# A selective scan on one core: TensorE makes the scan's input products from diagonals of B held in DRAM

## The chip, the cores and the metric

The kernel runs on one core of one Trainium2 chip. The metric is the device time of one execution in microseconds (us). The core has TensorE (PE in the profile, with PEld for its weight loads), VectorE (DVE), ScalarE (ACT), GpSimd (POOL) and SyncE (SP), which only issues DMAs here.

## The reference, cut to what matters

Two blocks follow each other over `x` of shape (2, 1024, 256): a conditioned linear layer that feeds a bidirectional Mamba block, and a conditioned linear layer that feeds a mixture of 8 experts, two for each token. The change touches only the scan of the Mamba block:

```python
x, z = (xz[..., :D_INNER], xz[..., D_INNER:])              # D_INNER = 512
x = silu(_causal_depthwise_conv(x, conv_w, conv_b))
x_dbl = x @ x_proj_w.T
dt = softplus(x_dbl[..., :DT_RANK] @ dt_proj_w.T + dt_proj_b)
Bm = x_dbl[..., DT_RANK:DT_RANK + D_STATE]                 # D_STATE = 16
Cm = x_dbl[..., DT_RANK + D_STATE:]
dA = jnp.exp(dt[..., None] * A)
dBx = (dt * x)[..., None] * Bm[:, :, None, :]              # the input products
h = dA_t * h + dBx_t                                       # the scan over time
y = jnp.einsum('bdn,bn->bd', h, C_t)                       # the output products and their sum
```

It is computed for two batches, forwards and backwards. Everything is float32.

## The kernel before, in words

**Units.** Channels lie on the 128 partitions, time along the free axis. The scan is cut into 256 units, `NU = NQ * SL`. `unit(i)` gives `q` (batch and direction, 4 values), `th` (half of the time axis, 512 steps), `pr` (a pair of the four channel blocks) and `n` (one of 16 states). A unit holds two channel blocks, `j` = 0 and 1, of 128x512 each. Sixteen units with the same `q`, `th`, `pr` are added up in the two PSUM banks `Y[0]` and `Y[1]` (`ps_y`), so there are 16 sums.

**What each engine does for a unit.** ScalarE (`decay`) makes two exponentials. VectorE makes the input product of block 0 into the bank `U` (`u`, L1068), runs the two scans (`second_scan` L1083 for block 1, `first_scan` L1096 for block 0), and in the units named in `OWN` also block 0's output product (`own_product`, L1108). GpSimd makes the input products of block 1 for two units at once (`u`, L1360, or L1356 for one) and the output products (`product`, L1376 for both blocks, L1372 for one). SP loads rows of B and C from the DRAM scratch `bc_scratch`, broadcast to 128 partitions, into a ring of three places of two units (`ring_load`). TensorE adds the output products up (`add`).

**Turned sums and flipped units.** For all but the last half of `q` = 3, `add_blocks` adds a product as four transposes of 128 columns for each block (L472): the bank holds the sum turned, with time on the partitions. At the end of a sum ScalarE copies it out (`evac_turned`), TensorE turns it back (`turn_back`, L465), and ScalarE copies it again (`evac`). The last half of `q` = 3 is `turned(q, th)` false: it adds with one plain product with the identity for each block (L470). In four units of 16 from unit 16 on, `flipped(i)`, neither VectorE nor GpSimd makes the input products: ScalarE scales the turned `dt * x` by columns of B (`u_turned`, L884, four instructions), and TensorE turns the result back into the banks (`second_u` L617, `first_u` L625).

**What sets the order.** Each engine's program is written out by hand as one loop over `i`. TensorE in iteration `i` does the turning, then `side_work(i)`, then `add(i - 2)` (`LAG` is 2). `side_work` is everything else TensorE has to do beside the scan: convolutions (L378), projections (L345, L354, L364, L386, L404, L417), and tiles of the next block (`tile`, `tile_T`, `tile_lg`, L439 to L458), each put at an iteration by a table (`STEP_AT`, `CONV_SLOTS`, `TILE_AT` and so on). Its results go through two PSUM banks, 6 and 7. VectorE's share of it is `small_work(i)`, behind the scans of unit `i`. Every queue is in order.

After the scan comes the expert stage: 39 tiles, with the products of 128 columns at L720 and of 256 columns at L731.

Of the kernel before, what the change touches and what calls it, by code (L numbers as in the profile page):

```python
# [21 lines left out]
FLIP, STRIDE = 6, 3  # L22
# [7 lines left out]
OWN = (6, 9, 12, 15, 22, 25, 28, 31)  # L30

NR, NH, NP, KD, LAG, EV, NW = 3, 5, 4, 6, 2, 4, 3


def at(q, s):
    return q * SL + s
# [3 lines left out]
STEP_AT = {3: (0, 0, 1), 22: (0, 1, 0), 36: (0, 1, 1), 54: (1, 0, 0), at(1, 3): (1, 0, 1),  # L40
           at(1, 22): (1, 1, 0), at(1, 36): (1, 1, 1), at(1, 42): (2, 0, 0), at(2, 1): (2, 0, 1),
           at(2, 18): (2, 1, 0), at(2, 33): (2, 1, 1), at(2, 46): (3, 0, 0), at(2, 59): (3, 0, 1),
           at(3, 8): (3, 1, 0), at(3, 27): (3, 1, 1)}


CONV_SLOTS = {1: (24, 26, 30, 32, 38, 40, 44, 46),
              2: (at(1, 10), at(1, 12), at(1, 16), at(1, 18), at(1, 24), at(1, 26), at(1, 30), at(1, 32)),
              3: (at(1, 59), at(1, 61), at(2, 21), at(2, 23), at(2, 27), at(2, 29), at(2, 36), at(2, 38))}
CONV_AT = {9 + 2 * m_: (0, m_, 1) for m_ in range(4)}
CONV_AT |= {i: (q_, g // 2, g % 2) for q_, slots in CONV_SLOTS.items() for g, i in enumerate(slots)}  # L50
XD_AT = {19: (0, 1), 50: (1, 0), 52: (1, 1), at(1, 38): (2, 0), at(1, 40): (2, 1), at(2, 42): (3, 0), at(2, 44): (3, 1)}
# [3 lines left out]
X1_AT = {0: (0, 1, 0), 1: (0, 1, 1), 56: (1, 0, 0), 57: (1, 0, 1), 59: (1, 1, 0), 60: (1, 1, 1)}  # L55
IN_AT = {5 + m_: (0, m_, 1) for m_ in range(4)}
IN_AT |= {i: (1, k // 2, k % 2) for k, i in enumerate((62, 63, at(1, 1), at(1, 2), at(1, 5), at(1, 6), at(1, 8), at(1, 9)))}

GATE_AT = {at(1, 44): (0, 1, 0), at(1, 45): (0, 1, 1), at(1, 49): (0, 1, 2), at(1, 50): (0, 1, 3),
           at(2, 3): (0, 0, 0), at(2, 4): (0, 0, 1), at(2, 8): (0, 0, 2), at(2, 9): (0, 0, 3),  # L60
# [3 lines left out]
LATE_AT = {at(2, 57): 0, at(2, 61): 1, at(3, 6): 2, at(3, 10): 3}  # L64
YG_AT = {g + 3: x for g, x in GATE_AT.items() if g + 3 < NU}
XT_AT = {at(1, 56): (0, 1), at(2, 15): (0, 0), at(3, 42): (1, 1), at(3, 55): (1, 0)}
XT_NO = {(0, 1): 2, (0, 0): 3, (1, 1): 4, (1, 0): 5}
OUT_AT = {at(1, 55): (0, 1, 0), at(1, 56): (0, 1, 1), at(2, 14): (0, 0, 0), at(2, 15): (0, 0, 1),
          at(3, 41): (1, 1, 0), at(3, 42): (1, 1, 1)}
TILE_AT = {at(2, 49): (0, 4), at(2, 53): (0, 5), at(2, 62): (0, 6), at(3, 2): (0, 7),  # L70
           at(3, 11): (0, 0), at(3, 15): (0, 1), at(3, 19): (0, 2), at(3, 23): (0, 3),
           at(3, 46): (1, 4), at(3, 50): (1, 5), at(3, 54): (1, 6), at(3, 58): (1, 7)}
# [4 lines left out]
def flipped(i):  # L77

    return i >= 16 and i % 16 >= FLIP and (i % 16 - FLIP) % STRIDE == 0


def flips(i):

    return sum(flipped(k) for k in range(i + 1))


def plain(i):

    return i + 1 - flips(i)


def swapped(i):

    return i + 1 < NU and flipped(i + 1)


NF = (15 - FLIP) // STRIDE + 1
DU_AT = {16 * g + 1 + j: (g, j) for g in range(1, 16) for j in range(2)}
ROWS_AT = {max(at(q_, 32 * h_), 16 * (1 - q_ - h_)) + 3: (q_, h_) for q_ in range(NQ) for h_ in range(2)}


def turned(q, th):

    return not (q == NQ - 1 and th)
# [8 lines left out]
def build(nc, d, out):  # L113
    ctx = ExitStack()
    with ctx:  # L115
# [25 lines left out]
        PS = Y + [DU, U] + DE + P2  # L141

        X_dram = nc.dram_tensor("X_scratch", (NB * T, C), F, kind="Internal").ap()
        bc_dram = nc.dram_tensor("bc_scratch", (NB * 2, 2 * NS, T), F, kind="Internal").ap()

        arena = sb("arena", [128, 43 * T + 8 * PAD + T + 64])
        am = Arena(arena)
# [135 lines left out]
        def own(i):  # L283

            return i % 32 in OWN

# [1354 lines left out]
```

## Time and profile before

| | us |
|---|---|
| median of 3 runs (1381.39 to 1389.28) | 1387.32 |
| the profiled execution | 1389.91 |
| its span, first to last instruction | 1388.1 |

| engine | busy us | share of the span |
|---|---|---|
| PE | 1228.0 | 88% |
| POOL | 918.5 | 66% |
| DVE | 899.6 | 65% |
| ACT | 777.4 | 56% |

The span has three parts: the start, up to the first scan at 41 us; the 256 units, up to about 916 us; and the experts, to the end. The shares above are averages over all three, and the stages have different limits. A record of a matmul has a duration of its own, but neighbouring matmuls overlap: the time that one takes from TensorE is read from the distance between the starts of groups, not from the mean duration.

### The profile page before, as it was taken

What the parts mean: (1) busy time and instruction counts of PE and PEld (TensorE: products, weight loads), DVE (VectorE), ACT (ScalarE), POOL (GpSimd) and SP (SyncE); (2) the same over time, 40 slices, a digit from 0 to 9 for tenths busy, and PEclk for the clock granted to TensorE, in tenths of its full rate; (3) what the DMA queues carried; (4) which work ended last, traced back from release to release, by engine and by line L of the source; (5) the groups of instructions that cost most, each with busy time, mean ns of one, the idle gap of its engine ahead of it and who ended that gap; (6) DMA issues with size and microseconds to landing.
All of it is one profiled execution on the core that took longest, in us unless ns stands there. A gap on an engine that the chain in (4) does not pass through costs nothing. (4 is left out here: it accounts for less than half of the span.)

```text
span 1388.1 us, 20902 instructions
## 1 busy us (share of the span) xinstructions
PE 1228.0 (88%) x7120; PEld 933.0 (67%) x7120; DVE 899.6 (65%) x1065; ACT 777.4 (56%) x1477; POOL 918.5 (66%) x511
## 2 busy tenths in 40 slices
PE   8978878989788879797787879898999999999997
PEld 3445555656556556566556644467999999999996
DVE  3998999899899899899998889963111111111110
ACT  4787887788887697788886675613111111111111
POOL 1998999999999989999998879822222222222211
PEclk9999999999999899899998799999999999999999
DMA  5665556465556455556555554608988898888982
GB/s 196 216 182 183 168 184 176 156 202 192 176 171 198 152 184 165 183 171 192 186 184 182 178 155 152 194 4 301 369 309 322 318 322 313 310 320 317 323 306 46
DMA packets 109979, 296.95 MB, mean 214 GB/s; under 512 B 10017, under 2 KB 21922, under 8 KB 94386
## 3 DMA queue, kind: packets, MB, share of 16 engines
q1 hardware_dynamic: 100226, 277.53, 57.9%
q0 software_dynamic: 9648, 18.09, 6.5%
q8 instruction: 57, 0.93, 0.3%
q14 instruction: 48, 0.39, 0.1%
HBM read 277.76 MB, written 9.96 MB: 207 GB/s over the span
## 5 line engine op out<-in xcount | busy, mean ns | idle before, releaser
L1376 POOL TENSOR_TENSOR arena<-arena 128x1024 f32<-128x1024 f32 x192 | 456.7, 2395 | 53.8 <-DVE arena L1096 38.2
L472 PE MATMUL ps_y<-ident,arena 128*128 128x128 f32 x1840 | 258.5, 289 | 54.0 <-POOL arena L1376 53.3
L472 PEld LDWEIGHTS ps_y<-ident,arena 128*128 128x128 f32 x1840 | 222.2, 148 | 121.8 <-POOL arena L1376 74.3
L1428 POOL DMA_INDIRECT out_x<-arena x39 | 61.8, 1585 | 304.9 <-ACT arena L1024 279.8
L871 ACT ACTIVATE arena<-arena,An 128x512 f32<-128x512 f32 x316 | 218.6, 710 | 0.1
L871 ACT ACTIVATE ps_de<-arena,An 128x512 f32<-128x512 f32 x196 | 134.9, 688 | 146.4 <-DVE arena L1083 140.4
L1310 DVE TENSOR_TENSOR arena<-ps_du,arena 128x512 f32<-128x512 f32 x39 | 27.0, 692 | 227.8 <-PE ps_du L720 227.8
L1360 POOL TENSOR_TENSOR arena<-arena 128x1024 f32<-128x1024 f32 x67 | 160.2, 2391 | 6.7 <-DMA arena<-bc_scratch 6.7
L720 PE MATMUL ps_y<-arena 128*128 128x128 f32 x1248 | 153.4, 276 | 0.8 <-ACT arena L1012 0.5
L720 PEld LDWEIGHTS ps_y<-arena 128*128 128x128 f32 x1248 | 149.6, 193 | 3.2 <-ACT arena L1012 0.8
L1068 DVE TENSOR_TENSOR ps_u<-ps_du,arena 128x512 f32<-128x512 f32 x196 | 136.8, 698 | 22.2 <-DVE arena L1108 10.1
L731 PE MATMUL ps<-arena 128*128 128x256 f32 x624 | 141.2, 379 | 0.5 <-issue 0.5
L731 PEld LDWEIGHTS ps<-arena 128*128 128x128 f32 x624 | 115.6, 190 | 15.0 <-issue 0.9
L1083 DVE TENSOR_TENSOR_SCAN arena<-ps_de,hlast,arena 128x512 f32<-128x512 f32 x96 | 121.8, 1269 | 5.1 <-ACT arena L871 3.8
L1083 DVE TENSOR_TENSOR_SCAN arena<-ps_de,arena 128x512 f32<-128x512 f32 x100 | 121.0, 1210 | 6.0 <-ACT arena L871 2.8
L1096 DVE TENSOR_TENSOR_SCAN arena<-arena,hlast,ps_u 128x512 f32<-128x512 f32 x96 | 121.3, 1263 | 4.3
L1096 DVE TENSOR_TENSOR_SCAN arena<-arena,ps_u 128x512 f32<-128x512 f32 x96 | 115.5, 1203 | 2.9
L1024 ACT ACTIVATE arena<-ps 128x256 f32<-128x256 f32 x39 | 15.0, 384 | 180.3 <-PE ps L731 171.9
L378 PE MATMUL ps<-arena 128*128 128x512 f32 x224 | 110.2, 615 | 0.4 <-ACT arena L807 0.3
L1018 ACT ACTIVATE arena<-ps_y 128x512 f32<-128x512 f32 x78 | 46.6, 597 | 113.7 <-PE ps_y L720 109.5
L1310 DVE TENSOR_TENSOR arena<-ps_u,arena 128x512 f32<-128x512 f32 x39 | 27.0, 692 | 120.7 <-PE ps_u L720 120.7
L884 ACT ACTIVATE arena<-arena 128x256 f32<-128x256 f32 x240 | 101.6, 496 | 0.0
(238 smaller groups left out, 2009.2 us busy)
## 6 DMA issues: line engine op xcount, KB each, us to landing
arena<-bc_scratch SPq DMA_DIRECT2D x256, 512.0 KB, 4.7
arena<-in_W SPq DMA_DIRECT2D x117, 1024.0 KB
arena<-arena POOLq DMA_DIRECT2D x15, 512.0 KB, 6.0
arena<-in_cd SPq DMA_DIRECT2D x16, 256.0 KB, 5.4
out_x<-arena SPq DMA_DIRECT2D x17, 128.0 KB, 5.0
arena<-in_xT SPq DMA_DIRECT2D x2, 1024.0 KB, 6.3
arena<-in_w2c SPq DMA_DIRECT2D x1, 2048.0 KB, 9.2
diag<-in_dd SPq DMA_DIRECT2D x16, 128.0 KB, 5.1
```

Of the source, the lines that this page charges most:

```text
L378: t = e.matmul(PS[p][:, :], cdiag[:, m % 2, k, :], xp[:, m, f:f + 512], start=(k == 0), stop=(k == KC - 1))
L472: t = e.matmul(Y[j][:, part], src[:, part], ident[:, :], start=False, stop=stop, is_transpose=True, skip_group_check=True)
L720: t = e.matmul(PS[o][:, j * 128:j * 128 + 128], w[:, i % NW, k, f:f + 128], xsT[:, i % 2, k, :], start=(k == 0), stop=(k == 1))
L731: t = e.matmul(PS[7][:, 0:C], hT[:, i % 2, k, :], w2[:, i % NW, k, :], start=(k == 0), stop=(k == 7))
L871: t = e.activation(to, dt[:, width_at(q, th, m), :], ACT.Exp, scale=An[:, q % 2, m, n:n + 1])
L884: t = e.activation(uT[:, k, :], duT[:, k, :], ACT.Copy, scale=bT[:, q % 2, th, k, f:f + 1])
L1068: e.tensor_tensor(U[:, :], DU[:, :], ring[:, turn % NR, 0, i % 2, :], ALU.mult).then_inc(dv_u, 1)
L1083: e.tensor_tensor_scan(h[:, 1, :], decay, x, hlast[:, 2 * pr + 1, n:n + 1] if th else 0.0, ALU.mult, ALU.add).then_inc(dv_sA, 1)
L1096: e.tensor_tensor_scan(U[:, :] if own(i) else h[:, 0, :], h[:, 0, :], U[:, :], hlast[:, 2 * pr, n:n + 1] if th else 0.0, ALU.mult, ALU.add ...
L1360: e.tensor_tensor(to, duA[:, 1:2, :].to_broadcast([128, 2, TH]), ring[:, turn % NR, 0, :, :], ALU.mult).then_inc(gp_u, 1)
L1376: e.tensor_tensor(hc[:, i % NP, :, :], hh[:, i % NH, :, :], c, ALU.mult).then_inc(gp_hc, 1)
L1428: e.indirect_dma_start(out, bass.IndirectOffsetOnAxis(dest[:, i:i + 1], 0), yo[:, i % 3, :], None, compute_op=ALU.add).then_inc(l_add, 16)
```

## The change

From unit 16 on (`FIRST`), no engine but TensorE makes input products. `make_u(i)` multiplies the turned `dt * x` (`duT`, time on the partitions) by a 128x128 matrix that has B of state `n` and 128 steps on its diagonal: four such products for each of the two blocks, into one of two pairs of banks, `S[i % 2]`. Both scans read their input there. `make_u(i + 2)` stands at the head of TensorE's iteration `i` and waits for the scans of unit `i`.

The diagonals come from a new DRAM scratch `dg_scratch`. At the start SP writes zeros into it (`put_zeros`, 16 DMAs of 512 KB), and for each half of each `q` four DMAs of 2048 single elements put the rows of B on the diagonals (`put_diagonals`). `load_b(i)` then loads the diagonals of a unit, 128x512, as many bytes as the broadcast rows took. B and C get rings of their own, six units each, loaded unit by unit.

VectorE's input product, GpSimd's input product, ScalarE's scaling and `second_u`/`first_u` are gone from unit 16 on. `OWN` is empty there: GpSimd makes both output products of every unit. In units 0 to 15 VectorE keeps four (`OWN_FIRST`). All sums are held unturned: `add` is one plain product with the identity for each block in every unit, as at L470; `evac_turned` and `turn_back` are gone. The turning of `dt * x` (`turn_du`) goes through the side banks. The tables of side work are new, with the same work in them.

```diff
-OWN = (6, 9, 12, 15, 22, 25, 28, 31)
+FIRST = 16
+OWN_FIRST, OWN = (3, 7, 11, 15), ()
...
+            def make_u(i):
+                g, k_ = i // 16, i - 2
...
+                e.wait_ge(dv_sA, k_ + 1)
+                e.wait_ge(dv_sB, k_ + 1)
...
+                rb_has(e, i)
+                for j in range(2):
+                    for k in range(4):
+                        t = e.matmul(S[i % 2][j][:, QUARTERS[k]], duT[:, g % 2, k, j * 128:j * 128 + 128],
+                                     rb[:, i % NRB, QUARTERS[k]], start=True, stop=True)
+                t.then_inc(pe_u, 1)
...
                 for j in range(2):
-                    t = add_blocks(q, th, j, hc[:, i % NP, j, :], n == 15)
+                    t = e.matmul(Y[j][:, :], ident[:, :], hc[:, i % NP, j, :], start=False, stop=(n == 15))
                 t.then_inc(pe_y, 1)
...
-                if not flipped(i):
+                if i < FIRST:
                     u(i)
...
-                if i % 2 == 0 and i + 2 < NU:
+                if i % 2 == 0 and i + 2 < FIRST:
                     u(i // 2 + 1)
...
+            def put_diagonals(q, th, k):
+                is_read(e, ("xd", q, th))
...
+                to = dg_dram[th].rearrange("n (p f) -> n p f", f=TH + 1)[:, :, k * 128]
+                src = xd[RK:RK + NS, th * TH + k * 128:th * TH + k * 128 + 128]
+                e.dma_start(to, src, allow_slow_non_contiguous=True).then_inc(l_dg, 16)
```

TensorE near units 27 to 32, before. L472 is the addition by transposes (x8 for the two blocks), L617 and L625 are the flipped unit's turning, L378 a convolution, L602 the turning of `dt * x`:

```order
L617 MATMUL ps_de<-ident,arena 128x128 x4
L472 MATMUL ps_y<-ident,arena 128x128 x8
L625 MATMUL ps_u<-ident,arena 128x128 x4
L378 MATMUL ps<-arena 128x512 x2
L472 MATMUL ps_y<-ident,arena 128x128 x8
L602 MATMUL ps_de<-ident,arena 128x128 x4
```

The same engine and place, after. L595 is `make_u` (x4 for each block), L491 the addition, L579 `turn_du`:

```order
L595 MATMUL ps_u<-arena 128x128 x4
L595 MATMUL ps_de<-arena 128x128 x4
L579 MATMUL ps<-ident,arena 128x128 x4
L491 MATMUL ps_y<-arena,ident 128x512 x2
L595 MATMUL ps_du<-arena 128x128 x4
L595 MATMUL ps_de<-arena 128x128 x4
```

Every unit now has eight plain products of 128 columns and two of 512, where most had eight transposes of 128 columns.

VectorE from unit 25 on, before. The names in capitals are the programs' own; SCALAR_TENSOR_TENSOR is the scan:

```order
L1104 COPY hlast<-ps_u 128x1
L1108 TENSOR_TENSOR arena<-ps_u,arena 128x512
L1068 TENSOR_TENSOR ps_u<-ps_du,arena 128x512
L1083 SCALAR_TENSOR_TENSOR arena<-ps_de,arena 128x512
L1096 SCALAR_TENSOR_TENSOR arena<-arena,ps_u 128x512
L1068 TENSOR_TENSOR ps_u<-ps_du,arena 128x512
L1096 SCALAR_TENSOR_TENSOR arena<-arena,ps_u 128x512
L1083 SCALAR_TENSOR_TENSOR arena<-ps_de,arena 128x512
```

VectorE in the same stage, after:

```order
L1023 SCALAR_TENSOR_TENSOR arena<-arena,ps_de 128x512
L1041 SCALAR_TENSOR_TENSOR arena<-arena,ps_du 128x512
L1023 SCALAR_TENSOR_TENSOR arena<-arena,ps_de 128x512
L1041 SCALAR_TENSOR_TENSOR arena<-arena,ps_u 128x512
L1023 SCALAR_TENSOR_TENSOR arena<-arena,ps_de 128x512
```

Only the scans are left, and block 0's input alternates between two banks.

## Rows read from the trace of the kernel before

**Rows 1.** Busy time by stretch: units 16 on, last 32 units, experts:

```profile
core 0: us, PE busy (x) PEld busy (x) DVE busy (x) ACT busy (x) POOL busy (x), PEclk, DMA share, GB/s
94.00:811.00 717.00, 590.30 (x3178) 411.29 (x3177) 655.14 (x709) 573.93 (x1081) 669.85 (x347) 0.92 0.58 179
811.00:913.00 102.00, 95.46 (x305) 47.31 (x304) 92.08 (x107) 54.95 (x102) 82.84 (x43) 0.99 0.45 148
1000.00:1300.00 300.00, 300.00 (x2272) 288.44 (x2271) 45.38 (x84) 53.98 (x110) 69.58 (x54) 1.00 0.89 316
```

**Rows 2.** Groups of DVE, 100 to 800 us: shapes, count | busy, mean ns | idle:

```profile
L1068 DVE TENSOR_TENSOR ps_u<-ps_du,arena 128x512 f32<-128x512 f32 x155 | 108.2, 698 | 19.0 <-DVE arena L1108 8.7 <-ACT ps_du L876 2.0 <-issue 0.5
L1083 DVE TENSOR_TENSOR_SCAN arena<-ps_de,arena 128x512 f32<-128x512 f32 x82 | 99.1, 1209 | 5.5 <-ACT arena L871 2.8 <-ACT ps_de L871 2.5 <-POOL arena L1360 0.2
L1083 DVE TENSOR_TENSOR_SCAN arena<-ps_de,hlast,arena 128x512 f32<-128x512 f32 x73 | 92.6, 1269 | 4.6 <-ACT arena L871 3.8 <-ACT ps_de L871 0.8
```

**Rows 3.** Groups of POOL in the same stretch:

```profile
L1376 POOL TENSOR_TENSOR arena<-arena 128x1024 f32<-128x1024 f32 x156 | 371.0, 2394 | 37.2 <-DVE arena L1096 27.2 <-DVE arena L1083 6.9 <-DMA arena<-bc_scratch 2.5
L1360 POOL TENSOR_TENSOR arena<-arena 128x1024 f32<-128x1024 f32 x53 | 126.6, 2388 | 5.9 <-DMA arena<-bc_scratch 5.9
```

**Rows 4.** Timeline of PE, early units: start, us, then the group:

```profile
44.22 3.67 PE L345 MATMUL ps<-arena,wmT 128*128 128x512 f32 x8 [0.98 <-DVE wbot L1049]
...
49.51 1.04 PE L472 MATMUL ps_y<-ident,arena 128*128 128x128 f32 x8
50.48 1.12 PE L386 MATMUL ps<-arena,dtT 16*128 16x512 f32 x2
51.53 1.09 PE L472 MATMUL ps_y<-ident,arena 128*128 128x128 f32 x8
```

**Rows 5.** Timeline of PE among the last 32 units, whose sums are plain:

```profile
860.74 0.60 PE L602 MATMUL ps_de<-ident,arena 128*128 128x128 f32 x4
861.18 1.88 PE L470 MATMUL ps_y<-arena,ident 128*128 128x512 f32 x4
862.90 1.03 PE L439 MATMUL ps<-wbot,arena 128*128 128x256 f32 x4
...
865.20 0.38 PE L458 MATMUL ps<-arena 1*128 1x8 f32 x2
865.51 1.98 PE L492 MATMUL ps_y<-arena,diag 128*128 128x512 f32 x4
```

**Rows 6.** Timeline of PE in the expert stage:

```profile
1103.74 1.95 PE L720 MATMUL ps_y<-arena 128*128 128x128 f32 x16
1105.53 1.95 PE L720 MATMUL ps_du<-arena 128*128 128x128 f32 x16
1107.31 0.38 PE L706 MATMUL ps_de<-ident,arena 128*128 128x128 f32 x2
```

**Rows 7.** All records of the plain sums (L470), with the count:

```profile
L470 PE MATMUL ps_y<-arena,ident x132: 592/592/841, 812.6 to 913.4; 128*128 128x512 f32 x132
```

**Rows 8.** Timeline of DVE where unit 16 begins:

```profile
94.14 1.22 DVE L1083 TENSOR_TENSOR_SCAN arena<-ps_de,arena 128x512 f32<-128x512 f32 x1 [0.52 <-POOL arena L1360]
95.28 1.20 DVE L1096 TENSOR_TENSOR_SCAN arena<-arena,ps_u 128x512 f32<-128x512 f32 x1
```

**Rows 9.** Timeline at the end of the last sum:

```profile
914.73 1.02 PE L510 MATMUL ps_y<-arena,ident 128*128 128x512 f32 x2
```

**Rows 10.** Waits, 100 to 800 us: us in total, times, longest us:

```profile
PE ps_y L472 <- POOL arena L1376: 45.6, 32, 5.0
DVE mx L1141 <- PE ps L458: 4.0, 2, 3.0
```

**Rows 11.** DMA queues and issues: packets, MB, share; KB each, us to landing:

```profile
q1 hardware_dynamic: 100226, 277.53, 57.9%
arena<-bc_scratch SPq DMA_DIRECT2D x256, 512.0 KB, 4.7
bc_scratch<-arena SPq DMA_DIRECT2D x2, 64.0 KB, 3.2
```

More of the change, by code:

```diff
@@ L73 @@
+TILE_AT = {at(2, 46): (0, 4), at(2, 47): (0, 5), at(2, 54): (0, 6), at(2, 55): (0, 7),
+           at(3, 6): (0, 0), at(3, 7): (0, 1), at(3, 14): (0, 2), at(3, 15): (0, 3),
+           at(3, 46): (1, 4), at(3, 47): (1, 5), at(3, 51): (1, 6), at(3, 52): (1, 7)}
 TILES = list(TILE_AT.values()) + [(1, i) for i in range(4)]
 TILE_NO = {x: k for k, x in enumerate(TILES)}
[L77 to L84, printed above, removed]
@@ L87, in plain @@
[L87 to L104, printed above, removed]
+DU_AT = {16 * g - 5 + j + (3 if g == 1 else g == 7): (g, j) for g in range(1, 16) for j in range(2)}
+CD_AT = {(slots[2 * m] - 4 if m < 2 else slots[2 * m - 3] + 7): (q_, m) for q_, slots in CONV_SLOTS.items() for m in range(4)}
@@ L283, in own, with rb_has, rc_has, made @@
         def own(i):
-            return i % 32 in OWN
+            return i in OWN_FIRST if i < FIRST else i % 32 in OWN
         def owned(i):
-            return i // 32 * len(OWN) + sum(k <= i % 32 for k in OWN)
+            return sum(own(k) for k in range(i + 1))
+        def rb_has(e, i):
+            e.wait_ge(l_rb[i % NRB], 16 * (i // NRB + 1))
+        def rc_has(e, i):
+            e.wait_ge(l_rcs[i % NRC], 16 * (i // NRC + 1))
+        def made(i):
+            return i - FIRST + 1
+        def cd_of(q, m):
+            return duT[:, 1, :, :].rearrange("p k (a f) -> p k a f", a=2)[:, :, m % 2, :] if q == 0 and m >= 2 else cdiag[:, m % 2, :, :]
+        def du_of(g):
+            return du1 if g == 1 else duA
         def cols_of(q, th):
@@ L635, in _ @@
+            for i in range(NU + LAG):
+                if FIRST <= i < NU - 2:
+                    if i == FIRST:
+                        make_u(i)
+                        make_u(i + 1)
+                    make_u(i + 2)
                 if i < NU:
                     side_work(i)
-                if i + 1 < NU and flipped(i + 1):
-                    second_u(i + 1)
                 if i == NU:
@@ L860, in decay @@
                         e.wait_ge(ac_hl, (i - NH) // SL * 32 + (i - NH) % SL + 1)
[L861 to L862 removed]
+                for j in (1, 0):
                     m = 2 * pr + j
                     to = hh[:, i % NH, j, :]
[L865 removed]
+                    if j and i < FIRST:
                         if i >= 2:
                             e.wait_ge(dv_sA, i - 1)
[L868 to L869 removed]
                         to = DE[i % 2][:, :]
@@ L897, in evac_turned @@
                     is_full(e, ("wb", NB - 1))
+                    if pr:
+                        for j in range(2):
+                            is_full(e, ("du", 1, j))
                 elif q == 2:
@@ L1508, in _ @@
             for i in range(NU + AHEAD):
-                if i < NU and i % 2 == 0:
-                    ring_load(i // 2)
+                if i == 0:
+                    load_b(0)
+                    load_b(1)
+                if i + 2 < NU:
+                    load_b(i + 2)
+                if i < NU:
+                    load_c(i)
+                if i in ZERO_AT:
+                    put_zeros(*ZERO_AT[i])
+                if i in SCATTER_AT:
+                    put_diagonals(*SCATTER_AT[i])
                 if i == 0:
                     sum_diag(0)
-                    for m in range(2):
+                    for m in range(4):
                         conv_diag(0, m)
```

370 lines of the change are left out of this document (159 added, 211 removed).

## The prediction

> **What bounds the kernel now.** I read the busy time by stretch first, because the page's shares mix stages. In the stretch from unit 16 to unit 223 VectorE is busy 655 of 717 us and GpSimd 670, both over 90%; TensorE shows 590, yet its records overlap, so that figure overstates what it has to do. In the expert stage TensorE is busy 300 of 300 us at a granted clock of 1.00 [rows 1]. The scan stage runs from unit 16's first scan at 94.1 us [rows 8] to the end of the last sum, 914.73 + 0.86 = 915.6 us [rows 9]: 821 us for 240 units, 3.42 us each. VectorE needs for a unit 0.70 + 1.21 to 1.27 twice, 3.2 us [rows 2], and GpSimd 2.39 for the output products and half of 2.39 for the input products, 3.6 us less what VectorE takes over [rows 3]. These two set the pace. TensorE waits for GpSimd (45.6 us at the additions alone) [rows 10]. So work taken off VectorE and GpSimd is worth something only up to what TensorE can do; the question is what TensorE has to do afterwards.
>
> **The price of a product on TensorE.** I take distances between starts. A plain product has two records: the last 33 units' 66 additions are 132 records [rows 7]. Four records of 512 columns, two additions, take 862.90 - 861.18 = 1.72 us, 0.86 each [rows 5]. Sixteen records of 128 columns take 1105.53 - 1103.74 = 1.79 us for eight products, 0.224 each, with weight loads that change every time and no gaps [rows 6]; `make_u` has this form exactly. A transpose has one record: four take 861.18 - 860.74 = 0.44 us, 0.11 each [rows 5]. A step width (L386) takes 51.53 - 50.48 = 1.05 us [rows 4]. A tile takes 865.51 - 862.90 = 2.61 us and its two later transposes 0.2, 2.8 in all [rows 5].
>
> **What is removed.** From unit 16 on VectorE loses 0.70 us a unit and the output products of its own, and is left with two scans, about 2.5 us. GpSimd loses 1.2 us a unit and gains the output products that VectorE had; it is left with 2.39 us. ScalarE loses the scaling and a second copy of each sum. All of this was at or near the bound, and would shorten the stage to 240 x 2.6 = 624 us if nothing else grew. TensorE loses the eight transposes of a turned unit, 8 x 0.11 = 0.88 us, and eight more in each flipped unit, 0.22 us a unit on average.
>
> **What is added to TensorE.** Each unit gets eight plain products of 128 columns, 1.79 us, and two plain additions of 512, 1.72 us: 3.51 us where 1.1 us stood. That alone is more than a unit takes today. Beside it stands the side work, which the change moves but doesn't lessen. For the whole scan stage, from TensorE's first side work at 44.2 us [rows 4]:
>
> - additions: 512 (two of 256 units) x 0.86 = 440 us
> - input products: 240 units x 1.79 = 430 us
> - other products of 512 columns: 112 of convolutions, 32 first terms of sums, 32 gates, 28 rows of B and C, 28 output blocks, 24 and 12 of the two input projections, 16 additions of the other direction; 284 x 0.86 = 244 us
> - 30 step widths x 1.05 = 32 us, 30 turnings of four transposes x 0.44 = 13 us, 12 tiles x 2.8 = 34 us
>
> The sum is 1193 us. Of this, 58 x 0.86 + 2 x 1.05 + 8 x 0.11 = 53 us lie in the iterations 0 to 15, and 1140 us behind them, 4.75 us for a unit. VectorE (2.5) and GpSimd (2.4) are then covered by TensorE. Iteration 16 can't begin before 44.2 + 53 = 97.2 us; the first 16 units run on the old path at about 3.3 us each and TensorE's additions wait for GpSimd, so I take 100 us. The end of the sums is then at 100 + 1140 = 1240 us, without any wait.
>
> **Waits that remain.** `make_u(i + 2)` waits for the scans of unit `i`. Its banks are two deep, so VectorE runs up to two units ahead, and the wait is normally over. I looked for places where VectorE waits for something of the same TensorE iteration. Two exist. (a) The top-two search of a tile (L1141) waits for `tile_lg` in iteration `t + 4`, already a wait now [rows 10]; only then can VectorE run the scans of unit `t + 5`, which TensorE needs at the head of its next iteration. That is 0.7 us of end and search plus 2.5 us of scans, against one pair of additions of 1.72 us: about 1.6 us, 12 times, 20 us. (b) `last_gated` in unit 241 waits for the sum that ends in the same iteration: 1.4 us of its own and 2.5 us of scans, 4 us once. The start of `make_u` (unit 18 waits for the scans of 16) costs 2 us. The copy of a sum by ScalarE stands three iterations behind `make_u`, one copy (about 0.6 us) and not two; the 1.79 us of `make_u` hide it. At nothing I also count the loads: the same bytes as before per unit, landing in 4.7 us [rows 11], asked for some five iterations, over 20 us, ahead. What waits on SP behind a late `load_b` are the loads of C. Where that cover fails is the second rival.
>
> **The DMAs.** The zeros are 16 x 512 KB = 8 MB, half of them in the first eight units; together with the loads of that time this is about 1 MB for 3.3 us, near the 316 GB/s that the expert stage reaches [rows 1]. I count 3 us. A `put_diagonals` moves 2048 single elements, which no row shows. Nearest from below is the write to the B and C scratch, 3.2 us to landing; from above, each element costs what an average packet of queue q1 does, 0.579 x 16 x 1388.1 / 100226 = 0.128 us, over 16 engines 2048 x 0.128 / 16 = 16.4 us [rows 11]. I take a value nearer the lower end, 5 us, since an element carries 4 bytes where the average packet carries 2.8 KB; four of them then end long before the diagonals are loaded. Such a DMA is made of one descriptor for each element and of writes under 512 bytes, and the Trainium skill warns of both ("DMA: Bandwidth & Descriptors", the sections "Rules for kernel authors" and "Specifications"): elements without a contiguous last dimension cost a descriptor each, and writes below 512 B are read, modified and written back. No row here shows either. By the same page's 10.5 ns a packet ("Measured", under "Bandwidth") one DMA would be 128 x 10.5 ns = 1.3 us, an estimate, and the sum would stay as it is.
>
> **A rule against this change.** The rows price the same 128 columns at 0.11 us as a transpose and 0.224 us as a plain product, a factor of two [rows 5, 6]. The Trainium skill ("TensorE: Matmul & The Clock Gate", section "Terms") calls the transpose mode four times faster for FP32. By it the plain additions would cost 3.5 us a unit and not 1.72, and the time would be some 450 us longer still. The plain additions have rows of their own, so the measured factor stands, and I give the other no chance.
>
> **The sum.** End of the sums: 100 + 1140 + 20 + 4 + 2 + 3 = 1269 us. What follows it, 1388.1 - 915.6 = 472.5 us, is unchanged. Span 1741.5 us; the profiled execution lay 1.8 us over its span and 2.6 us over the median, so I say **1740 us**, 25% more than now. The granted clock should be near 1.00 in the stage, as in the experts, against 0.92 now [rows 1]; the distances above were all taken at full clock.
>
> **The rivals.**
>
> - *Slower by more: the diagonals come late.* At 16.4 us each, four take 66 us. Before unit 16 they are issued near 61 us (after the product of unit 4) and wanted near 98: 29 us of waiting. For each of the seven later halves 66 us and some 23 us of ordinary loads stand against about 16 iterations of 4.75 us: 13 us each, 91 in all. The time would be 1740 + 120 = 1860 us. Against it: the element's small size. It decides from about 12 us a DMA on.
> - *Slower by a little more: gaps between kinds of work.* `make_u` has five waits and stands between two other kinds. If each of its 240 turns, and each addition, left 0.1 to 0.2 us open, that is 50 to 100 us: 1790 to 1840 us. Against it: the expert stage also mixes three kinds with waits and shows no idle time in 300 us.
> - *Faster: TensorE hides the products.* VectorE then sets the pace at 2.6 us a unit, and the time is 1388 - (821 - 624) = 1190 us. That needs TensorE below 2.6 us a unit; it breaks even where TensorE needs 3.4 us. It would take plain products at the price of transposes (8 x 0.11 + 8 x 0.11 and half of the side work, 2.4 us). The rows of both kinds speak against it.
> - *The change doesn't do what it says* (no input products on TensorE, or fewer): the program's order shows 240 times eight products, so I give this nothing.
>
> **How the numbers follow.** My forecast, TensorE as the bound with few waits: 0.80, between 1708 (44.2 + 1193 + 472.5 = 1709.7, the sum with no waits at all, less 2) and 1790. Gaps: 0.10. Late diagonals: 0.08. Faster: 0.015; something between: 0.005. The range that holds 8 in 10 is 1708 to 1810: the floor is hard, and above it takes in the smaller gaps. About 0.5% is what a measurement of this kernel can tell from no change; slower by more than that has 0.98, the rest 0.005 and 0.015.
>
> **What would show it.** TensorE busy for nearly all of the stage from 100 to 1270 us, at clock 1.00; VectorE busy about 60% and GpSimd 50%, waiting for L595; L595 with 3840 records, 16 of them in 1.79 us; the pace of scans 4.7 to 4.9 us a unit. SP waiting long for `dg_scratch`, or TensorE's L595 waiting for a DMA, would speak for late diagonals; idle time of TensorE ended by "issue" for gaps. A pace below 4.2 us would say that the price of a plain product is wrong, and with it the whole prediction.

## The result, and the profile after

| | us |
|---|---|
| median of the changed kernel, 4 runs (1774.55 to 1786.78) | 1778.99 |
| median of the kernel before, 4 runs beside it (1381.12 to 1389.28) | 1384.36 |
| ratio, with its 95% interval | 1.285 (1.279 to 1.292) |
| the profiled execution, and its span | 1786.78, 1785.0 |

The kernel is 28.5% slower. The forecast was 1740 us, in a range of 1708 to 1810.

The busy time by stretch, as in [rows 1]: busy us of each engine with its number of records, then TensorE's granted clock, the share of the DMA engines, GB/s. The stretches are the first units, the middle of the scan, and the experts:

```profile
40.00:100.00 60.00, 40.69 (x86) 16.40 (x86) 38.10 (x43) 29.64 (x56) 35.92 (x18) 0.86 0.82 176
300.00:500.00 200.00, 200.00 (x958) 128.34 (x957) 99.69 (x84) 87.68 (x162) 104.90 (x47) 1.00 0.62 124
1400.00:1700.00 300.00, 300.00 (x2272) 288.44 (x2271) 46.01 (x84) 54.29 (x111) 71.97 (x56) 1.00 0.89 316
```

In the middle of the scan TensorE is busy for 200 of 200 us at a clock of 1.00; VectorE is down to 50% and GpSimd to 52%, from over 90% both [rows 1]. The bound has moved from two engines to a third that now has more to do than either had. The experts are as before. The first stretch is another matter: there TensorE is busy for only two thirds of the time, while the DMA engines show 0.82.

TensorE's timeline at 500 us (start and duration in us, then the group and its number of records), to be laid beside [rows 5, 6]:

```profile
500.33 1.05 PE L595 MATMUL ps_du<-arena 128*128 128x128 f32 x8
501.22 1.06 PE L595 MATMUL ps_de<-arena 128*128 128x128 f32 x8
502.11 1.02 PE L481 MATMUL ps_y<-arena,ident 128*128 128x512 f32 x2
502.97 1.88 PE L491 MATMUL ps_y<-arena,ident 128*128 128x512 f32 x4
504.69 1.05 PE L595 MATMUL ps_u<-arena 128*128 128x128 f32 x8
505.58 1.06 PE L595 MATMUL ps_de<-arena 128*128 128x128 f32 x8
506.57 1.12 PE L386 MATMUL ps<-arena,dtT 16*128 16x512 f32 x2
507.62 1.13 PE L491 MATMUL ps_y<-arena,ident 128*128 128x512 f32 x2
```

The eight products of `make_u` take 502.11 - 500.33 = 1.78 us, an addition 0.86, a step width 1.05. TensorE is never idle ahead of any of these groups (idle time would be in brackets at the end of a line).

Groups from 100 to 1300 us (count | busy, mean ns | idle before, with what ended it), and the waits of the other engines in the same stretch (us in total, times, longest):

```profile
L1314 POOL TENSOR_TENSOR arena<-arena 128x1024 f32<-128x1024 f32 x244 | 576.0, 2362 | 541.2 <-PE ps_y L491 303.9 <-DVE arena L1041 226.7 <-DMA arena<-bc_scratch 9.7
L595 PE MATMUL ps_de<-arena 128*128 128x128 f32 x1920 | 255.2, 276 | 0.0
L595 PE MATMUL ps_du<-arena 128*128 128x128 f32 x960 | 128.2, 277 | 13.7 <-issue 9.6 <-DMA arena<-dg_scratch 3.1 <-ACT arena L812 1.0
L595 PE MATMUL ps_u<-arena 128*128 128x128 f32 x960 | 126.8, 275 | 2.1 <-issue 2.1
```

```profile
POOL arena L1314 <- PE ps_y L491: 303.9, 115, 5.8
DVE arena L1023 <- PE ps_de L595: 216.1, 91, 9.6
DVE mx L1086 <- PE ps L458: 56.3, 12, 7.1
```

`make_u` has 1920 + 960 + 960 = 3840 records, 240 units of 16, and 15.8 us of idle time ahead of them in all, 3.1 us of it for the diagonals. GpSimd waits for TensorE to read its products, VectorE for TensorE to make its inputs.

The stage itself lies between two lines of TensorE's timeline, the first `make_u` and the last addition of the last sum:

```profile
134.42 0.80 PE L595 MATMUL ps_du<-arena 128*128 128x128 f32 x5 [0.98 <-ACT arena L812]
...
1307.53 1.02 PE L486 MATMUL ps_y<-arena,ident 128*128 128x512 f32 x2
```

From 134.42 to 1307.53 + 0.86 = 1308.4 us are 1174.0 us; behind that 476.6 us are left to the end of the span. The forecast had 1166 us for the same stretch (1140, 20, 4 and 2), 472.5 behind it, but 103 us ahead of it (100, and 3 for the zeros). Of the 43.5 us by which the span passes the forecast's 1741.5, 31.4 lie before unit 16, 8 in the stage and 4.1 behind it. These are figures of the profiled execution, the slowest of the four and 7.8 us above their median.

**Where the 31 us before unit 16 are.** SP's timeline: start, how long the issue took, the DMA issued. L1457 is `put_diagonals`, L1429 the load of B (or of diagonals), L1438 that of C:

```profile
67.08 0.66 SPq L1457 DMA_DIRECT2D dg_scratch<-arena  x1
67.88 1.31 SPq L1429 DMA_DIRECT2D arena<-bc_scratch  x1
69.30 0.58 SPq L1438 DMA_DIRECT2D arena<-bc_scratch  x1
70.40 0.60 SPq L1457 DMA_DIRECT2D dg_scratch<-arena  x1
71.06 8.50 SPq L1475 DMA_DIRECT2D diag<-in_dd  x1
...
80.61 0.56 SPq L1457 DMA_DIRECT2D dg_scratch<-arena  x1
81.27 9.02 SPq L1429 DMA_DIRECT2D arena<-bc_scratch  x1
90.38 0.38 SPq L1438 DMA_DIRECT2D arena<-bc_scratch  x1
90.86 0.56 SPq L1457 DMA_DIRECT2D dg_scratch<-arena  x1
91.52 10.17 SPq L1429 DMA_DIRECT2D arena<-bc_scratch  x1
```

Behind each of these four `put_diagonals` but the first, whatever DMA comes next takes 8.5 to 10.2 us to issue, where its neighbours take 0.4. The blocked DMAs are a load for the next sum and the ordinary rows of B of units 12 and 13; the rows of B from unit 11 on and of C from unit 9 on stand behind them in the queue. On VectorE and TensorE the same time looks like this (in brackets the idle time before the group, and what ended it):

```profile
91.63 1.22 DVE L1023 TENSOR_TENSOR_SCAN arena<-ps_de,arena 128x512 f32<-128x512 f32 x1 [12.55 <-POOL arena L1300]
112.78 0.69 DVE L1053 TENSOR_TENSOR arena<-ps_u,arena 128x512 f32<-128x512 f32 x1 [15.59 <-DMA arena<-bc_scratch]
```

The first wait is for GpSimd's input product of units 10 and 11, which itself waits for rows of B; the second is for the row of C of unit 11.

```profile
94.98 3.78 PE L491 MATMUL ps_y<-arena,ident 128*128 128x512 f32 x4 [14.35 <-POOL arena L1314]
116.88 3.78 PE L491 MATMUL ps_y<-arena,ident 128*128 128x512 f32 x4 [11.96 <-POOL arena L1314]
```

TensorE's additions wait for GpSimd, GpSimd and VectorE for rows that SP can't issue. Another queue is delayed as well. GpSimd issues a DMA of its own that adds up step widths (L1328), and waits for it before it can make more input products (L1282); this wait, in the changed kernel and then in a_nodiag below, which has no element DMAs:

```profile
109.89 2.34 POOL L1282 TENSOR_TENSOR arena<-arena 128x1024 f32<-128x1024 f32 x1 [12.66 <-DMA arena<-arena]
86.08 2.34 POOL L1282 TENSOR_TENSOR arena<-arena 128x1024 f32<-128x1024 f32 x1 [3.95 <-DMA arena<-arena]
```

GpSimd's 15 DMAs of this kind land in 9.1 us (median; the slowest in 18.3) beside element DMAs, and in 5.5 us (9.6) without.

The additions behind these waits also take longer, 3.78 us for two where [rows 5] have 1.88, because after 14 us of idling TensorE runs at the lower of its two clock levels, 1.2 GHz; the stretch of the first of them:

```profile
95.00:99.00 4.00, 4.00 (x5) 1.81 (x6) 2.16 (x3) 3.96 (x6) 2.23 (x1) 0.50 0.47 31
```

The diagonals of unit 16 are not late: what releases its `make_u` at 134.4 us is the copy of the turned `dt * x` (ACT L812).

**Late diagonals, once.** The four element DMAs of the second half, at 153 to 177 us, block SP for 8.3 to 9.2 us at a time too. There the load of the diagonals does come late; the wait, and TensorE's clock in the 9.3 us behind it:

```profile
193.86 2.05 PE L595 MATMUL ps_du<-arena 128*128 128x128 f32 x8 [3.11 <-DMA arena<-dg_scratch]
193.80:203.10 9.30, 9.24 (x23) 5.50 (x23) 2.33 (x2) 2.58 (x5) 4.96 (x3) 0.50 1.03 386
```

The wait costs 3.1 us, and the work behind it, at half the clock, 4.7 us more than its price at full clock. Both are part of the 1174.0 us.

### The profile page after: what moved, and what is told of

It is laid out like the page before. It is cut to its first block, busy times and chain, and to the rows that moved or that the text cites. A ratio compares the mean times of both kernels' runs of the same rounds, so it can differ in the third digit from the quotient of the medians.

```text
span 1785.0 us, 24949 instructions
## 1 busy us (share of the span) xinstructions
PE 1718.7 (96%) x9248; PEld 1231.2 (69%) x9248; DVE 742.8 (42%) x797; ACT 659.3 (37%) x1186; POOL 776.4 (43%) x392
## 3 DMA queue, kind: packets, MB, share of 16 engines
q1 hardware_dynamic: 175490, 286.20, 57.0%
## 4 chain that ended last, share of the span: by engine, by line
PE 91%; SPq 3%; DMA 2%; issue 1%; ACT 1%; DVE 1%; POOL 0%; POOLq 0%; DVEq 0%; ACTq 0%
PE ps_y L491 24%; PE ps_de L595 12%; PE ps_y L688 8%; PE ps L699 7%; PE ps_du L595 6%; PE ps_u L595 6%; PE ps L378 5%; PE ps_u L688 4%; PE ps_du L688 4%; PE ps L386 2%; PE ps_y L471 2%; SPq L1429 2%; PE ps L404 2%; PE ps L364 1%; PE ps L417 1%
## 5 line engine op out<-in xcount | busy, mean ns | idle before, releaser
L491 PE MATMUL ps_y<-arena,ident 128*128 128x512 f32 x1020 | 490.1, 603 | 28.7 <-POOL arena L1314 28.7
L491 PEld LDWEIGHTS ps_y<-arena,ident 128*128 128x128 f32 x1020 | 183.5, 192 | 236.7 <-issue 189.2
L1023 DVE TENSOR_TENSOR_SCAN arena<-arena,hlast,ps_de 128x512 f32<-128x512 f32 x128 | 163.4, 1277 | 239.6 <-issue 177.0
L595 PE MATMUL ps_de<-arena 128*128 128x128 f32 x1920 | 255.2, 276 | 0.0
L1023 DVE TENSOR_TENSOR_SCAN arena<-arena,ps_de 128x512 f32<-128x512 f32 x112 | 136.4, 1218 | 248.0 <-PE ps_de L595 216.1
L595 PEld LDWEIGHTS ps_de<-arena 128*128 128x128 f32 x1920 | 235.2, 193 | 0.0
L595 PEld LDWEIGHTS ps_du<-arena 128*128 128x128 f32 x960 | 126.0, 193 | 73.7 <-issue 71.3
L595 PEld LDWEIGHTS ps_u<-arena 128*128 128x128 f32 x960 | 125.8, 192 | 60.7 <-issue 56.4
L595 PE MATMUL ps_du<-arena 128*128 128x128 f32 x960 | 128.2, 277 | 13.7 <-issue 9.6
L595 PE MATMUL ps_u<-arena 128*128 128x128 f32 x960 | 126.8, 275 | 2.1 <-issue 2.1
L378 PE MATMUL ps<-arena 128*128 128x512 f32 x224 | 104.5, 599 | 0.0
## 6 DMA issues: line engine op xcount, KB each, us to landing
arena<-in_xT SPq DMA_DIRECT2D x2, 1024.0 KB, 10.5
```

What stands on the lines that cost most here:

```text
L378: t = e.matmul(PS[p][:, :], cd_of(q, m)[:, k, :], xp[:, m, f:f + 512], start=(k == 0), stop=(k == KC - 1))
L491: t = e.matmul(Y[j][:, :], ident[:, :], hc[:, i % NP, j, :], start=False, stop=(n == 15))
L595: t = e.matmul(S[i % 2][j][:, QUARTERS[k]], duT[:, g % 2, k, j * 128:j * 128 + 128], rb[:, i % NRB, QUARTERS[k]], start=True, stop=True)
L1023: e.tensor_tensor_scan(h[:, 1, :], decay, x, hlast[:, 2 * pr + 1, n:n + 1] if th else 0.0, ALU.mult, ALU.add).then_inc(dv_sA, 1)
```

## Experiments

All medians are of 4 runs, beside 1384 to 1389 us for the kernel before. "Main part" in the table is the time from the start of the first scan of unit 32 to the start of the first scan of unit 255, the last, 223 units, read from VectorE's timeline of the profiled execution; "unit 32" is when that first scan starts.

| kernel | median us | ratio to before (95%) | unit 32 | main part |
|---|---|---|---|---|
| before | 1387 | | 150.2 | 758.7 |
| changed | 1779.0 | 1.285 (1.279 to 1.292) | 216.5 | 1080.1 |
| a_nodiag | 1754.2 | 1.264 (1.260 to 1.269) | 184.8 | 1081.1 |
| a_spread | 1761.5 | 1.273 (1.269 to 1.278) | 193.7 | 1078.4 |
| a_own | 1785.7 | 1.289 (1.284 to 1.294) | 218.8 | 1083.3 |
| b_plain | 1410.0 | 1.019 (1.015 to 1.023) | 153.0 | 770.9 |
| a_turned | 1649.8 | 1.190 (1.185 to 1.195) | 211.8 | 946.4 |
| a_turned_rows | 1604.2 | 1.156 (1.151 to 1.161) | 171.4 | 939.6 |
| a_two | 1511.7 | 1.093 (1.089 to 1.098) | 202.9 | 815.8 |
| a_two_rows | 1440.4 | 1.038 (1.035 to 1.041) | 165.9 | 785.4 |
| a_two_turned | 1453.0 | 1.051 (1.047 to 1.055) | 202.1 | 764.2 |
| a_two_turned_rows | 1362.3 | 0.982 (0.978 to 0.986) | 158.3 | 711.6 |
| v1 | 1504.3 | 1.085 (1.079 to 1.092) | 168.9 | 847.1 |
| v1_rows | 1402.1 | 1.010 (1.007 to 1.014) | 154.8 | 765.3 |

My theory was that TensorE bounds the stage and that its work adds up record by record; the rivals were gaps between kinds of work, late diagonals, and an engine other than TensorE.

**a_nodiag: the element DMAs replaced.** Each of the 32 `put_diagonals` writes as many bytes, in 16 runs:

```diff
-                to = dg_dram[th].rearrange("n (p f) -> n p f", f=TH + 1)[:, :, k * 128]
+                to = dg_dram[th][:, k * 128:k * 128 + 128]
```

> The changed kernel, but each of the 32 DMAs that put B on the diagonals writes its 16 x 128 values as 16 runs of 512 bytes, and not as 2048 single elements; the rest of the computation runs on wrong input products, so this part is left out. The zeros are still written. If the single elements (about 9.7 us a DMA in the trace, in the queue of the ring's loads) made units 0 to 15 last 35 us longer than forecast, the time falls to 1745 us. If the 8 MB of zeros did it, it stays above 1770 us. If late diagonals also cost time in the later halves, it falls below 1735 us.

It measured 1754.2 us, 25 less, between the 1745 of the first theory and the 1770 of the second. SP's timeline at the same place has no blocked issue:

```profile
69.06 0.32 SPq L1457 DMA_DIRECT2D dg_scratch<-arena  x1
69.44 0.40 SPq L1475 DMA_DIRECT2D diag<-in_dd  x1
...
70.88 0.38 SPq L1457 DMA_DIRECT2D dg_scratch<-arena  x1
71.36 0.36 SPq L1429 DMA_DIRECT2D arena<-bc_scratch  x1
```

and TensorE's first `make_u` begins 24 us earlier:

```profile
110.56 1.13 PE L595 MATMUL ps_du<-arena 128*128 128x128 f32 x8 [0.98 <-ACT arena L812]
```

So 24 of the 31 us are the four element DMAs of the first half. (These are times of the profiled executions, whose spans lie 30.6 us apart; the medians lie 25 apart.) The four of the second half cost 8 us more: from the first `make_u` to the first scan of unit 32 this kernel takes 184.8 - 110.6 = 74.2 us and the changed one 216.5 - 134.4 = 82.1 us, which is the late load of diagonals and the slow clock behind it. The 24 after them cost nothing, since the main part stays the same, 1081.1 against 1080.1 us. Without element DMAs the stage lasts 1277.6 - 110.6 = 1167.1 us. The other 7 us before unit 16 were not split; no run leaves out the zeros.

**a_spread: the same DMAs put further apart.** The zeros of the first half go ahead of the first scan, the four `put_diagonals` stand at units 2, 6, 10 and 13 and not at 7 to 10:

```diff
-SCATTER_AT = {i_: (0, 0, k) for k, i_ in enumerate((7, 8, 9, 10))}
+SCATTER_AT = {i_: (0, 0, k) for k, i_ in enumerate((2, 6, 10, 13))}
```

> The changed kernel with the same DMAs at other places of SP's program: the first eight DMAs of zeros ahead of the first scan and not beside units 0 to 7, and the first four DMAs of diagonals beside units 2, 6, 10 and 13 and not 7 to 10. If the ring's loads queue behind single elements (9.7 us each, four in 13 us of work), spreading them gives back 10 to 25 us: about 1762 us. If the total of DMA work in the first 16 units is the limit, it stays at 1779 us.

1761.5 us, as the first part of the expectation has it. With no less work, only by other places, 17.5 of the 25 us come back. It is the fastest kernel with the whole change that also computes everything, and still 27% slower than the kernel before.

**a_own: VectorE takes output products.** `OWN = ()` becomes the list of before:

```diff
-OWN_FIRST, OWN = (3, 7, 11, 15), ()
+OWN_FIRST, OWN = (3, 7, 11, 15), (6, 9, 12, 15, 22, 25, 28, 31)
```

> The changed kernel with the output products of block 0 given back to VectorE in eight of 32 units (OWN as before), 60 of the units from 16 on: VectorE gets some 0.86 us more in each, GpSimd 1.1 us less. If TensorE alone sets the pace, VectorE has over 2 us of room a unit and the time stays at 1779 us, within 6. If VectorE's scans are on the path (each make_u waits for them), it rises by up to 60 x 0.86 = 52 us.

1785.7 us, 6.7 more by the medians, just outside the 6 of the expectation and far from its 52. The single runs overlap (1783.5 to 1792.3 here, 1774.6 to 1786.8 in the changed kernel), and the main part is 3 us longer. Who makes the output products matters little; VectorE's scans are not what sets the pace.

**b_plain: one part alone, in the kernel before.** All sums plain, nothing else: `turned(q, th)` always false and the two steps of turning back left out.

```diff
-    return not (q == NQ - 1 and th)
+    return False
```

> The kernel before with only the other part of the change: its sums are held unturned everywhere, input products as they were. TensorE's work in the scan stage rises from 619 us by 188 + 5 - 12 to 800 us, of 871 us that the stage lasts. If only a full engine costs time, the kernel stays within 15 us of 1384. If TensorE's answers to VectorE and ScalarE get late before it is full (the turnings of flipped units queue behind longer additions), it gets slower by 20 to 80 us.

1410.0 us, 23 more, at the low end of what the second theory gives. Busy time from 100 to 900 us, b_plain:

```profile
100.00:900.00 800.00, 759.51 (x2246) 349.78 (x2245) 716.85 (x778) 601.17 (x1125) 723.26 (x375) 1.00 0.56 174
```

and before:

```profile
100.00:900.00 800.00, 670.07 (x3418) 450.13 (x3418) 729.82 (x796) 619.88 (x1164) 737.46 (x382) 0.92 0.57 178
```

TensorE is busier by 89 us and has 41 to spare; the kernel is slower all the same. It fits that an engine which is not yet full already costs time where others wait for it: VectorE's wait for the flipped unit's input (`ps_u`, L625) is 25.3 us here and 6.3 us before.

**a_turned: the changed kernel with turned sums again.** `add_blocks`, `turn_back` and `evac_turned` of the kernel before come back into the changed kernel.

```diff
-                    t = e.matmul(Y[j][:, :], ident[:, :], hc[:, i % NP, j, :], start=False, stop=(n == 15))
+                    t = add_blocks(q, th, j, hc[:, i % NP, j, :], n == 15)
```

> The changed kernel with one part undone: the sums of all but the last half are held turned again, so an addition is eight transposes (0.88 us a unit) in place of two plain products of 512 columns (1.72 us). Input products stay on TensorE. If TensorE's own work sets the pace, 224 units give back 0.84 us each, 188 us, and 12 additions of the other direction 5 us; the turning back costs 14 x 0.88 = 12 us and a wait for the two copies of a sum about 1 us each, 14 us. That makes 1779 - 167 = 1612 us. If something else sets the pace (the waits between the engines, the loads), it stays above 1740 us.

1649.8 us, between the two expectations. 129 us come back where the prices promise 167.

**a_two: a quarter of the input products.** From unit 18 on only the first of the four products of each block is made; the other three quarters of the input are left out.

```diff
-                    for k in range(4):
+                    for k in range(1 if i >= FIRST + 2 else 4):
```

> The changed kernel, but from unit 18 on make_u makes only the first of four products for each block, two of eight; the scans read old values in the other three quarters, so this part of the computation is left out. All waits stay. If TensorE's own work sets the pace, 238 units give back 6 x 0.224 = 1.34 us each, 320 us: 1779 - 320 = 1459 us, a pace of 3.4 us a unit. If the round trip between scans and make_u sets it, or VectorE and GpSimd do, less comes back and the time stays above 1500 us.

1511.7 us: 267 of 320 us, which the expectation gives to the second theory (above 1500); the trial without element DMAs below shows that most of the missing 53 us are not the round trip.

**a_two_turned: both.** It leaves out the same.

> Both at once: sums held turned and two of eight products made (the rest left out). TensorE then has about 1139 - 320 - 171 = 648 us for 240 units, 2.7 us a unit, VectorE two scans of 1.2 to 1.28 us, 2.5 us a unit, GpSimd 2.4. If the engines' own work adds up as forecast, 1650 - 320 = 1330 us, and TensorE and VectorE are about level; if waits grow as engines get level (turned sums gave back 129 us where 167 were expected), 1350 to 1400 us. That is about what would be left to gain if the products cost TensorE next to nothing.

1453.0 us, above both expectations, 326 us back where the prices promise 487. With most of its input products left out the kernel is still 5% slower than before. Here the rows show what the sum of prices lacks. TensorE's waits for the diagonals, 100 to 900 us:

```profile
PE ps_u L625 <- DMA arena<-dg_scratch: 41.6, 9, 7.6
...
PE ps_du L625 <- DMA arena<-dg_scratch: 9.4, 4, 6.2
```

These are 51 us, against 3.1 in the changed kernel. So the element DMAs that cost the changed kernel nothing behind unit 32 may be what is missing here. Three kernels test it.

**a_turned_rows, a_two_rows, a_two_turned_rows: the same three without element DMAs** (the edit of a_nodiag in each).

> a_turned with each put_diagonals writing 16 runs of 512 bytes in place of 2048 single elements (the input products are wrong for that). Turned sums gave back 129 us where the prices say 167. If the 38 us that are missing are the cost of the element DMAs in later halves, which TensorE hid in the changed kernel and hides no longer, this kernel comes to 1754 - 167 = 1587 us, 63 us below a_turned. If the missing part is small waits of engines that are nearly level, the same edit gives only the 25 us that it gave in the changed kernel: 1625 us.

> a_two with the same replacement, so plain sums, a quarter of the input products from unit 18 on (three of four products of each block are left out) and none of the element DMAs. A quarter of the products gave back 267 us where the prices say 320. By the first theory, element DMAs in the later halves, 1754 - 320 = 1434 us; by the second, small waits of engines that are nearly level, 1512 - 25 = 1487 us.

> a_two_turned with the same replacement (16 runs of 512 bytes for 2048 single elements), so a kernel with turned sums, a quarter of the input products and none of the element DMAs. a_two_turned was 1453 us, and its units from 16 on took about as long as those of the kernel before; its loss lay in the first 16 units. If the element DMAs cost only in the first 16 units, as in the changed kernel itself, the gain is the 25 us that the same edit gave there: 1428 us. If they cost in the later halves too, now that TensorE no longer hides what waits there, it is 60 us or more: 1393 us or less.

They measured 1604.2, 1440.4 and 1362.3 us, that is 46, 71 and 91 us less, where the edit gave 25 in the changed kernel: the less TensorE has to do, the more the element DMAs cost. For a_two_rows the first theory of its expectation holds (1440 against 1434 us), for a_two_turned_rows the second, costs in the later halves too (1362 against 1393 or less). a_turned_rows, 1604 us, lies between the two (1587 and 1625). Measured from a_nodiag, the turned sums alone give 150 of 167 us, the quarter of the products 314 of 320, and both together 392 of 487. The element DMAs thus explain 21 of the 38 us that a_turned lacked, 47 of 53 for a_two and 66 of 161 for a_two_turned. a_two_turned_rows is the one kernel that beats the kernel before, by 1.8%, and it leaves out three quarters of the input products and holds wrong ones for the rest; it is no version to use. What it lacks beyond the element DMAs (95 us) has another ground. No engine is full in it (200 to 800 us):

```profile
200.00:800.00 600.00, 542.16 (x3194) 397.98 (x3193) 462.52 (x433) 425.09 (x752) 487.25 (x216) 0.96 0.65 193
```

It takes 711.6 / 223 = 3.19 us for a unit, where TensorE needs 2.7 by the prices (4.75 - 1.34 - 0.70) and VectorE 2.5. From 100 to 900 us VectorE waits 113.4 us for ScalarE's exponentials (L864, 69 times) and GpSimd 121.6 us for VectorE's scans, and nothing waits long for a DMA. That it is the round trip between engines fits these waits, but no run separates it.

**v1: the change cut to the flipped units.** The kernel before, in which the four flipped units of 16 get their input from diagonals and no longer from ScalarE's scaling; turned sums, ring and `OWN` stay, but a place of the ring with a flipped unit is filled by three DMAs and not two.

```diff
-                    t = e.transpose(U[:, QUARTERS[k]], uT[:, k, 0:128], ident[:, :])
+                    t = e.matmul(U[:, QUARTERS[k]], duT[:, k, 0:128], ring[:, i // 2 % NR, 0, i % 2, QUARTERS[k]],
+                                 start=True, stop=True)
```

> The kernel before with only its flipped units (four of 16) made from diagonals: TensorE multiplies the turned dt times x by the diagonals of B from DRAM, where ScalarE scaled and TensorE turned back. Sums stay turned, all else as before. TensorE gets 60 x (1.79 - 0.88) = 55 us more, 674 of 871 us; ScalarE loses 240 instructions of 0.5 us, 119 us. ScalarE is not at its bound, so from that little comes back: 1384 us, within 20. If the 32 DMAs of single elements hold up the ring's loads (9.7 us each against a lead of some 13 us), it rises by 20 to 80 us.

1504.3 us: 117 more than before, outside both expectations. Waits from 100 to 900 us:

```profile
POOL arena L1369 <- DMA arena<-bc_scratch: 40.9, 15, 7.0
...
POOL arena L1365 <- DMA arena<-bc_scratch: 25.6, 11, 7.1
...
DVE ps_u L1077 <- DMA arena<-bc_scratch: 20.4, 13, 3.9
```

The first two are GpSimd's input products, which before waited 6.1 us in all for their rows (L1360). v1 has the same 32 element DMAs, and a ring of three places that is soon empty.

**v1_rows: v1 without element DMAs** (again the edit of a_nodiag).

> v1 with each put_diagonals writing 16 runs of 512 bytes in place of 2048 single elements (the input products of the flipped units are wrong for that; all else is as in v1). v1 was 117 us slower than the kernel before. Theory A: the element DMAs do it: 32 of them take about 9.7 us each of the queue that also carries the ring's loads, while a ring of three places is only about 20 us ahead, so that VectorE and GpSimd wait for rows of B and C in all halves. Then this kernel comes back to 1390 to 1420 us. Theory B: the diagonals do it through TensorE: 60 flipped units with 8 products of 0.224 us instead of 8 transposes of 0.11 us, 54 us more in all, late in a chain that VectorE waits for, and one load of 256 KB more in each turn that has a flipped unit. Then it stays at 1470 to 1505 us.

1402.1 us, as theory A has it. 102 of the 117 us are the element DMAs. The wait for the rows has gone with them:

```profile
POOL arena L1365 <- DMA arena<-bc_scratch: 4.0, 7, 0.9
POOL arena L1369 <- DMA arena<-bc_scratch: 3.9, 7, 0.8
```

and the time from issue to landing of `put_diagonals` (the last number; before it the count and the bytes) falls from

```profile
dg_scratch<-arena SPq DMA_DIRECT2D x32, 8.0 KB, 12.1
```

in v1 to

```profile
dg_scratch<-arena SPq DMA_DIRECT2D x32, 8.0 KB, 4.6
```

in v1_rows. The remaining 15 us hold what 60 flipped units pay for plain products, 54 us of TensorE's time, partly hidden; the zeros and the loads that are split in two are in them too, and no run separates them.

## Why the prediction was right, and where it was off

- **The bound, and the prices.** Right. The prices came out as read from the rows of before: `make_u` 1.78 us against 1.79, an addition 0.86, a step width 1.05. The stage took 1174 us where 1166 were forecast, and 1167 in a_nodiag. The pace of the main part is 1080.1 / 223 = 4.84 us a unit, forecast 4.7 to 4.9. VectorE is busy 50% (forecast 60%; 2.5 us of 4.8 would have said 52) and GpSimd 52%. One reading was off without effect: the 132 records of [rows 7] are the 66 additions of 31 units and four of the other direction, not of 33 units; it is two records for each all the same.
- **When iteration 16 begins: the step that failed.** The sum took 100 us, and 3 for the zeros; it was 134.4. It had nothing for the element DMAs: I took 5 us for a `put_diagonals`, "a value nearer the lower end, 5 us, since an element carries 4 bytes where the average packet carries 2.8 KB". SP's next issue is held for 8.5 to 10.2 us, between the bounds of 3.2 and 16.4 and not near the lower one. The Trainium skill's 10.5 ns a packet ("DMA: Bandwidth & Descriptors", "Measured" under "Bandwidth"), from which I made the estimate of 1.3 us, was further off still; the page takes it from a load of 64 packets out of HBM, issued by GpSimd, and not from single elements written to DRAM. What the same page says of a last dimension that isn't contiguous ("Rules for kernel authors"), one descriptor for each element, agrees with the trace: queue q1 has 175490 packets in the changed kernel and 110466 in a_nodiag, 65024 fewer, 32 x (2048 - 16), one for each element.
- **What such a DMA delays.** Here the prediction had the mechanism wrong. It looked for diagonals that come late, at unit 16 and in the later halves, from 12 us a DMA on. At unit 16 they were in time; what came late were the ordinary rows of B from unit 10 and of C from unit 9 on, issued behind the element DMAs on the one queue, and GpSimd's own DMA on another. I had counted "What waits on SP behind a late `load_b`" but not what waits behind `put_diagonals`. In the second half the diagonals were late once, at 9 us a DMA and not 12, and that cost 8 us with the slow clock behind it. Behind unit 32 a busy TensorE hides all of it. Where it doesn't (a_two_turned), TensorE does wait for diagonals, 51 us.
- **What was luck.** The 1174 us for the stage are so near to 1166 because errors cancel: the three waits that I counted, 26 us, came to about 13, and the late diagonals (3), the slow clock (8) and the small gaps (12), which I put at nothing, make up for that.
- **Waits in the stage.** The 20 us for tiles were too many, and the 2 us at the start of `make_u` came to 0.8 (139.0 us). VectorE waits 56.3 us at the top-two search (12 times), but TensorE is idle for only about 8 us near the tiles, by the distances between the starts of its records: VectorE mostly has scans in hand when it begins to wait. `last_gated` was forecast at 4 us and shows this line, in unit 241:

```profile
1239.64 1.13 PE L595 MATMUL ps_du<-arena 128*128 128x128 f32 x8 [3.79 <-issue]
```

- **Gaps between kinds of work.** All distances between starts in the stage, less the price of each record, leave 35 us: 3.8 here, some 8 at tiles, 3.1 for diagonals once (at 193.9 us), some 8 more because TensorE ran at half the clock for 9 us behind that wait and for 6 behind the one shown here, and the other 12 in small pieces over 240 units, 0.05 us each. The rival asked for 50 to 100.
- **The clock.** As forecast in all of the stage but these two stretches, which bring it to 0.99; 0.979 over the span.
- **The tail.** 476.6 us against 472.5. This part of the time varies between the profiled executions, whatever the change: 472.5 us before, 476.7 in b_plain (1407.3 - 930.6), 469.2 in a_spread, 471.2 in a_own, 473.2 in v1_rows. So the 4.1 us can't be put down to the input products; their cause was not looked into.
- **The break-even.** The prediction said that the change breaks even "where TensorE needs 3.4 us" a unit. a_two_rows needs 4.75 - 1.34 = 3.41 us by the prices. Its main part takes 3.52 us a unit, before 3.40; with 16 us lost up to unit 32, it is 4% slower. So the estimate was 0.1 us a unit too kind. Below that point, at 2.7 us by the prices, a unit takes 3.19.

## What to carry to other kernels

Before work is moved to an engine that looks half idle, price the new form from rows of that engine and add up all that it will have to do: here the sum with its few waits gave 1166 us where 821 stood, and 1174 were measured (1167 without the element DMAs). Such a sum is right for the engine that is full; it overstates what comes back when work is taken off until two or three engines are level. A DMA of many tiny elements must be priced by the other DMAs that are wanted while it runs, those behind it on its queue above all, and a trial with the same bytes in long runs shows its cost at once; a bound elsewhere can hide that cost, and it returns (25 us, then 46, 71, 91) as the bound is removed.

## What the runs showed of the hardware that I had not expected

- Before unit 16 a DMA of 2048 single elements of 4 bytes holds its queue for 8.5 to 10.2 us, in the mean of the three rows 9.2 us. If the elements are spread evenly over 16 DMA engines, that is 72 ns for each of 128, an estimate. Behind the same 8 KB in 16 runs of 512 bytes the next issue takes 0.4 us (a_nodiag), and they land in 4.6 us against 12.1 (v1_rows and v1). Whether the number of pieces or their size makes the difference, no run separates.
- It slows the DMAs of another queue too: GpSimd's DMA for the step widths, issued at 91.5 us, lands in 18.3 us; the slowest of its kind without element DMAs takes 9.6.
- TensorE's clock was granted at 0.50 for the 9.3 us behind a wait of 3.1 us, after it had been at 1.00 with TensorE busy without a gap for 50 us; that cost 4.7 us, more than the wait.
- Thirty-two such DMAs made a kernel that is otherwise 1% slower than before 8.5% slower.
- b_plain loses 1.9% although TensorE, after the added work, has 5% of its time free at full clock.
